# Five graph layers in one program: the next pass's weights and first rows prepared in the last groups of the pass ahead, and three steps of VectorE in another order

## The chip, the core and the metric

One Trainium2 chip, of which the program uses one core. Its engines are TensorE (PE), VectorE (DVE), ScalarE (ACT), GpSimd (POOL) and SyncE (SP); SP only issues DMA transfers here. The metric is the device time of one execution in microseconds (us), lower is better.

## What is computed

`x` has 128 graphs of 64 nodes with 384 features, fp32; `adj` is 128 x 64 x 64. Four layers follow one another, each `x = layernorm(x + layer(x, adj))`:

```python
# layer 0 and layer 3: attention with 12 heads, a bias from adj, an output projection
scores = einsum(q, k) * scale + bias            # bias = adj + adj in layer 0, adj in layer 3
p = softmax(where(any(scores != 0), scores, -inf)); out = einsum(p, v) @ Wo.T + bo
# layer 1: masked attention, with row biases for q, k, v, no output projection
scores = where(adj > 0, einsum(q, k) / sqrt(32) + beta * adj, -9e15)
out = einsum(softmax(scores), v)
# layer 2: twice (two sets of weights), then the residual and layernorm of the layer
attn = normalised(softmax(h @ h.T / sqrt(384)) * adj)
ctx = (attn * upper) @ (h @ Wl.T + bl) + diag(attn) * (h @ Ws.T + bs) + (attn * lower) @ (h @ Wr.T + br)
h = relu(layernorm(ctx) * g + b)
```

## The kernel before

The 8192 rows (128 graphs x 64 nodes) are 16 groups of 512 rows; a group is four units of 128 rows, two graphs each. The program runs five passes over all rows, each storing its result to HBM for the next: l0 (attention), l1 (masked attention), l20 and l21 (the two halves of layer 2, `digcn_pass`; only l21 has `ends`, the layer's residual and second norm), and l3 (attention). l0 and l3 are the same code with `wo`, the output projection; l1 has none.

Each fp32 operand of a large product is held in two parts, a rounded high part and the rest, and each product is three matmuls over these (`SPLIT`). For the rows: DVE transposes 128 x 512 tiles from `xa` to `xF` (L743 in the attention passes, L1363 in the digcn passes), ACT makes the high part (L591, L1239), POOL the low part (L379, L1099), three tiles a group. For the weights, nine tiles of 128 x 384 in each pass: DVE transposes them out of `raw` (L727, L1348; not in l1, whose weights come in the right form), ACT makes the high part (L583, L1231), DVE the low part (L733, L1352).

A pass is one block with a queue written by hand for each engine; `over_groups` calls `group` for the 16 groups, and writes the first two and the last two out. Order on an engine is that of the code; engines wait for one another by semaphores that count. At its start a pass of before fetches and splits the rows of groups 0 and 1 and its weights; it ends with a barrier of all engines (L883, L1529), behind which the next pass begins. The raw weights of the next pass are fetched by DMA in the pass ahead.

In an attention pass the projections of group i+1 stand on PE between the steps of group i (`BETWEEN`). One unit's chain is: PE scores (L478); DVE adds the bias (L770), takes the maximum (L777) and, with `wo`, the minimum (L779); POOL subtracts (L396); ACT takes the exponential (L663); DVE sums (L784); PE transposes (L491) and multiplies with v (L512 or L516). With `wo`, ACT and DVE split the outcome into oT (L817 is its low part), PE multiplies by Wo (L531), and DVE adds the residual (L828) with the statistics (L832, L835). Without `wo`, DVE scales (L813), POOL adds the residual (L373). `normed` on ACT, three instructions, makes the normalised row in all three passes.

In l1 DVE also makes the bias of the next group in unit 2 (`edges`: L757, L759), and POOL adds the bias of v (L354).

In a digcn pass PE multiplies the rows with themselves (L1152) for the attention of group i+1, and projects LEFT, RIGHT and SELF for each unit (L1179). DVE's `attention` has steps 0 to 4; step 3 is L1397 and L1403, whose outcome `wide` PE transposes (L1163); step 4 is L1408 and L1410. All of them are for the next group and stand in units 1 to 3. `context` on DVE is L1432 (in l21), L1437, L1440; `itself`, in l20 only, is L1417, which empties the SELF bank. POOL's L1106 adds the row biases of the LEFT and RIGHT projections. In l21 the bias of SELF is a row that ACT rounds (L1301, L1302), DVE splits (L1489) and PE adds (L1185).

## Time and profile before

| | |
|---|---|
| time before, median of 3 runs | 2734.35 us (2733.89 to 2734.68) |
| profiled execution, its own time | 2734.95 us |
| its span, mean granted clock | 2733.2 us, 0.964 |
| busy over the span: PE, DVE, ACT, POOL | 90%, 73%, 62%, 72% |

Time is in microseconds from the span's start. A clock of 1.00 is 2.4 GHz, one of 0.50 is 1.2 GHz. The engine's idle time in a row is that just before the instruction, and the releaser is what ended it; a row with "x3" stands for three instructions with nothing else between them on that engine. SPq rows are the issues of DMA transfers. The passes run, roughly, from 24 to 636 us (l0), 640 to 1175 (l1), 1180 to 1591 (l20), 1595 to 2100 (l21) and 2105 to the end (l3).

### The profile page before, as it was taken

The page shows a single profiled execution, that of the slowest core. Times are in us where ns is not written, and L with a number is a line of the kernel's source. Part 1 is how long each engine was busy: PE and PEld are TensorE (multiplying, and loading weights), DVE is VectorE, ACT ScalarE, POOL GpSimd, SP SyncE. Part 2 cuts the span into 40 slices and gives each one's busy share as a digit, 9 for nine tenths or more (in the row PEclk, how much of TensorE's full clock was granted, in tenths as well). Part 3 has the DMA queues.
Part 4 walks back from the last instruction along what each step waited for, and adds up shares of the span by engine and source line. Part 5 has one row for each costly group of instructions (what it writes and reads, how often), then busy time and mean ns, then how long its engine had stood idle before and what let it go on. Part 6 is the DMA issues. An engine that isn't in the chain of part 4 may idle for free. (4 is left out here: it accounts for less than half of the span.)

```text
span 2733.2 us, 65211 instructions
## 1 busy us (share of the span) xinstructions
PE 2471.4 (90%) x21554; PEld 2108.1 (77%) x21554; DVE 1992.3 (73%) x3475; ACT 1689.4 (62%) x3606; POOL 1969.1 (72%) x2189
## 2 busy tenths in 40 slices
PE   6999999985999999869999968888885999999997
PEld 4888888874877777758888857777774888888886
DVE  4777777773677667668888858888787577777776
ACT  4667666664777777745454445555654576666665
POOL 3888788873777777756666647777775588878786
PEclk9999999997999999979999989999997999999998
DMA  7222223115233332172333163333324222232211
GB/s 128 62 71 70 70 65 73 44 50 101 69 84 80 79 81 67 55 129 63 75 73 69 39 120 75 92 79 79 79 70 91 53 69 71 68 72 68 59 46 50
DMA packets 320602, 200.71 MB, mean 73 GB/s; under 512 B 243426, under 2 KB 320484, under 8 KB 320484
## 3 DMA queue, kind: packets, MB, share of 16 engines
q1 hardware_dynamic: 320484, 199.21, 31.6%
q8 instruction: 66, 1.08, 0.2%
q14 instruction: 52, 0.43, 0.1%
HBM read 136.22 MB, written 62.91 MB: 73 GB/s over the span
## 5 line engine op out<-in xcount | busy, mean ns | idle before, releaser
L1179 PE MATMUL l_ps_h<-l_w,l_hT 128*128 128x384 f32 x3456 | 672.0, 347 | 2.3 <-issue 2.3
L457 PE MATMUL l_ps_p<-l_xT,l_w 128*128 128x512 f32 x2304 | 598.3, 407 | 83.3 <-POOL l_xT L379 76.8
L1179 PEld LDWEIGHTS l_ps_h<-l_w,l_hT 128*128 128x128 f32 x3456 | 614.9, 193 | 63.3 <-issue 54.0
L457 PEld LDWEIGHTS l_ps_p<-l_xT,l_w 128*128 128x128 f32 x2304 | 426.3, 191 | 179.8 <-DVE l_w L733 51.7
L784 DVE TENSOR_REDUCE l_st<-l_pr 128x12 f32<-128x768 f32 x192 | 182.9, 953 | 348.7 <-ACT l_pr L663 348.7
L396 POOL TENSOR_TENSOR l_pr<-l_sc,l_st 128x768 f32<-128x768 f32 x192 | 285.1, 1485 | 172.2 <-DVE l_st L777 172.2
L1261 ACT ACTIVATE l_hlr<-l_ps_h 64x384 f32<-64x384 f32 x512 | 248.8, 486 | 196.8 <-PE l_ps_h L1179 190.0
L354 POOL TENSOR_TENSOR v<-v,l_bvs 128x768 f32<-128x768 f32 x192 | 356.2, 1855 | 0.0
L1106 POOL TENSOR_TENSOR l_hlr<-l_hlr,l_sides 128x768 f32<-128x768 f32 x128 | 246.7, 1928 | 125.6 <-ACT l_hlr L1261 125.4
L451 PE MATMUL l_ps_p<-l_w,l_xT 128*128 128x384 f32 x1584 | 312.6, 342 | 15.7 <-ACT v L622 14.8
L451 PEld LDWEIGHTS l_ps_p<-l_w,l_xT 128*128 128x128 f32 x1584 | 272.6, 188 | 25.3 <-ACT v L622 18.8
L531 PE MATMUL l_ps_y<-l_w,l_oT 128*128 128x384 f32 x1152 | 234.1, 348 | 43.7 <-DVE l_oT L817 39.9
L622 ACT ACTIVATE v<-l_ps_p 64x192 f32<-64x192 f32 x704 | 228.0, 324 | 55.0 <-PE l_ps_p L451 47.3
L531 PEld LDWEIGHTS l_ps_y<-l_w,l_oT 128*128 128x128 f32 x1152 | 205.7, 192 | 66.9 <-issue 63.4
L379 POOL TENSOR_TENSOR l_xT<-l_xF,l_xT 128x512 fp32r<-128x512 f32 x144 | 184.0, 1291 | 85.8 <-ACT l_xT L591 85.8
L405 POOL TENSOR_TENSOR l_pr<-l_pr,l_st 128x768 f32<-128x768 f32 x128 | 188.6, 1473 | 69.5 <-DVE l_st L795 69.5
L663 ACT ACTIVATE l_pr<-l_pr 128x768 f32<-128x768 f32 x192 | 162.2, 845 | 116.8 <-POOL l_pr L396 115.9
L770 DVE SCALAR_TENSOR_TENSOR l_sc<-l_ps_s,l_sbias 128x768 f32<-128x768 f32 x192 | 183.6, 956 | 34.0 <-PE l_ps_s L478 27.8
L777 DVE TENSOR_REDUCE l_st<-l_sc 128x12 f32<-128x768 f32 x192 | 183.0, 953 | 6.6
L658 ACT ACTIVATE l_pT<-l_ps_t 128x512 f32<-128x512 f32 (+1 forms) x384 | 167.4, 490 | 19.7 <-PE l_ps_t L491 13.7
L478 PE MATMUL l_ps_s<-l_k,l_qT 64*64 64x128 f32 x4608 | 172.7, 281 | 5.9 <-DVE l_sc L770 5.9
L478 PEld LDWEIGHTS l_ps_s<-l_k,l_qT 64*64 64x64 f32 x4608 | 125.7, 134 | 64.7 <-issue 58.0
(138 smaller groups left out, 4383.6 us busy)
## 6 DMA issues: line engine op xcount, KB each, us to landing
rows<-l_yo SPq DMA_DIRECT2D x256, 192.0 KB, 1.9
l_xa<-rows SPq DMA_DIRECT2D x256, 192.0 KB, 4.3
l_xr<-rows SPq DMA_DIRECT2D x192, 192.0 KB, 2.4
l_xa<-in_x SPq DMA_DIRECT2D x64, 192.0 KB, 4.3
l_xr<-in_x SPq DMA_DIRECT2D x64, 192.0 KB, 2.3
out<-l_yo SPq DMA_DIRECT2D x64, 192.0 KB, 1.9
l_edge<-in_adj SPq DMA_DIRECT2D x80, 128.0 KB, 2.4
raw<-in_L_gnn_Wq SPq DMA_DIRECT2D x12, 144.0 KB, 4.9
```

What stands on the lines that cost most here:

```text
L354: nc.gpsimd.tensor_tensor(got, got, bvs[:, :, :].unsqueeze(1).to_broadcast([P, GPU, PAIRS, 64]), ALU.add).then_inc(pool_v, 1)
L379: nc.gpsimd.tensor_tensor(xT[gpar][:, 1, t, :], xF[:, t, :], xT[gpar][:, 0, t, :].bitcast(F32), ALU.subtract).then_inc(low_x, 1)
L396: nc.gpsimd.tensor_tensor(pr[b][:, :, :], sc[b][:, :, :], st[b][:, 0, :].unsqueeze(2).to_broadcast([P, HEADS, NODES]), ALU.subtract).then_ ...
L405: nc.gpsimd.tensor_tensor(pr[b][:, :, :], pr[b][:, :, :], st[b][:, 5, :].unsqueeze(2).to_broadcast([P, HEADS, NODES]), ALU.mult).then_inc( ...
L451: last = nc.tensor.matmul(bank[:, :D], rows[:, l, t, o * P:(o + 1) * P], W[2][:, r, t, :], start=c + t == 0, stop=c == 2 and t == KT - 1)
L457: last = nc.tensor.matmul(bank[:, :], W[m][:, l, t, o * P:(o + 1) * P], rows[:, r, t, :], start=c + t == 0, stop=c == 2 and t == KT - 1)
L478: last = nc.tensor.matmul(logits[g * NODES:(g + 1) * NODES, h:h + 2, :NODES], qT[par][q, t, c:c + NODES], k2[par][q, t, :, c:c + NODES], s ...
L531: last = nc.tensor.matmul(ps_y[:, :D], oT[b][:, l, t, :], W[3][:, r, t, :], start=c + t == 0, stop=c == 2 and t == KT - 1)
L622: i = nc.scalar.activation(v2[gpar][64 * odd:64 * odd + 64, GPU * u + g2, :, 32 * odd:32 * odd + 32], got[:, :, odd, :], ACT.Copy)
L1106: nc.gpsimd.tensor_tensor(hlr[b][:, :, :], hlr[b][:, :, :], sides[:, :, :], ALU.add).then_inc(pool_h, 1)
L1179: last = nc.tensor.matmul(ps_h[m][:, :D], hT[gpar][:, l, t, s * P:(s + 1) * P], W[m][:, r, t, :], start=c + t == 0, stop=not (ends and m = ...
L1261: i = nc.scalar.activation(hlr[b][half * NODES:(half + 1) * NODES, g, :], ps_h[m][g * NODES:(g + 1) * NODES, :D], ACT.Copy)
```

## The change

What both kinds of pass share now lies in `Shared`: `W`, `xa`, `xF` (double-buffered in the attention passes too), `xT`, and the semaphores of this work, whose counts run on through all passes. A `Feed` describes what a pass is fed with: its rows, its weights, and the counts at its start.

- Rows. Groups 16 and 17 of a pass are groups 0 and 1 of the next. They are fetched, transposed and split in the usual places of groups 14 and 15. A pass from the second on no longer fetches or splits its first rows (of the six tiles all are done for l1 and l20; for l21 and l3 five are transposed and three split, the rest follow at the start).
- Weights. In the last group of an attention pass the nine tiles of the next pass are done three to a unit: DVE's transposes behind the softmax sum of units 0 to 2 (none for l1), ACT's high parts and DVE's low parts in units 1 to 3, with the banks of the projections. In a digcn pass each unit of groups 14 and 15 does one tile, the last unit two: DVE transposes at the unit's end, ACT follows, and DVE makes the low part at the head of the next unit. The two digcn passes have weight buffers of their own in turn. Wo stays where it was, at the start of l0 and l3.
- In l0 and l3 the minimum stands behind oT's low part in every unit.
- In l1 `normed` is one DVE instruction behind `low_part`, in place of three on ACT.
- In the digcn passes step 3 of `attention` stands ahead of `context` (l21) and of `itself` (l20). Step 4 stays.
- In l21 the rounding of the bias row is counted by its own semaphore.

```diff
+        self.W = [sb(f"w{m}", [P, 2, KT, D], F32R) for m in range(4)]
+        self.xa = [sb(f"xa{b}", [P, 4 * UNITS, D // 4]) for b in range(2)]
+        self.xF = [sb(f"xF{b}", [P, KT, ROWS]) for b in range(2)]
+        self.xT = [sb(f"xT{b}", [P, 2, KT, ROWS], F32R) for b in range(2)]
+        self.s_xa = [nc.alloc_semaphore(f"s_xa{b}") for b in range(2)]
+        self.dve_turn, self.act_x, self.low_x, self.dve_wt, self.act_w, self.dve_w = (
+            nc.alloc_semaphore(x) for x in ("dve_turn", "act_x", "low_x", "dve_wt", "act_w", "dve_w"))
...
+class Feed:
+
+
+    def __init__(self, k, src, mats, turned, W, turned_before, tiles_turned, tiles_split):
+        self.k, self.src_x, self.mats, self.turned, self.W = k, spread(src), mats, turned, W
+        self.rows_base, self.w_base, self.wt_base = KT * 16 * k, 3 * KT * k, 3 * KT * turned_before
+        self.tiles_turned, self.tiles_split = tiles_turned, tiles_split
...
+        def next_bank(step):
+            return (*ps_p, ps_y)[step % 3][:, :]
+
+        def has_rows(g):
+            return inside(g, groups + (2 if nxt else 0))
...
             def rows_in(g, gpar):
-                if not inside(g, groups):
-                    return
-                if counted(g - 1):
-                    sp.wait_ge(dve_turn, KT * (g - 1))
+                if not has_rows(g):
+                    return
+                if counted(rb + KT * (g - 1)):
+                    sp.wait_ge(dve_turn, rb + KT * (g - 1))
                 for j in range(4):
-                    sp.dma_start(xa[gpar][32 * j:32 * j + 32, :, :], src_x[g, j]).then_inc(s_xa[gpar], 16)
-
-            rows_in(0, 0)
-            rows_in(1, 1)
+                    part = nxt.src_x[g - groups, j] if isinstance(g, int) and g >= groups else me.src_x[g, j]
+                    sp.dma_start(xa[gpar][32 * j:32 * j + 32, :, :], part).then_inc(s_xa[gpar], 16)
+
+            if me.k == 0:
+                rows_in(0, 0)
...
-            shared.load(sp, next_mats, next_turned, lambda m: sp.wait_ge(dve_w, KT * min(m + 1, NM)))
+            if nxt:
+                shared.load(sp, nxt.mats, nxt.turned, lambda m: sp.wait_ge(dve_w, wb + KT * min(m + 1, 3)))
...
-            for step in range(KT):
-                weight_high(step)
+            if me.k == 0:
+                for step in range(KT):
+                    weight_high(me, step, w_bank(step))
             for t in range(KT):
                 rows_high(0, 0, t)
-            for step in range(KT, 3 * KT):
-                weight_high(step)
+            if me.k == 0:
+                for step in range(KT, steps):
+                    weight_high(me, step, w_bank(step))
             if row_bias_cols:
...
             def normed(n, count, b):
 
-                if not inside(n, units):
+                if not inside(n, units) or not wo:
...
+                    if nxt and s and isinstance(i, int) and i == groups - 1:
+                        act.wait_ge(pe_p, 10 * groups)
+                        for step in range(KT * (s - 1), KT * s):
+                            weight_high(nxt, step, next_bank(step))
...
+            def softmax_min(n, s):
+                b = s % 2
                 if wo:
                     nc.vector.tensor_reduce(st[b][:, 1, :], sc[b][:, :, :], AX.X, ALU.min).then_inc(dve_mn, 1)
...
+            def normed(n, count, b):
+                if not inside(n, units) or wo:
+                    return
+                dve.wait_ge(pool_rs, n + 1)
+                dve.wait_ge(dve_mv, n + 1)
+                if counted(16 * count):
+                    dve.wait_ge(s_out[b], 16 * count)
+                nc.vector.tensor_scalar(yo[b][:, :], res[b][:, :], ln[b][:, 6:7], ln[b][:, 9:10], ALU.subtract,
+                                        ALU.mult).then_inc(ready_y, 1)
...
+            if me.k == 0:
+                for t in range(KT):
+                    weight_turned(me, t, w_bank(t), 4)
+                for t in range(KT):
+                    weight_low(me, t, w_bank(t))
...
                     residual(n - 3, count, 1 - s % 2)
                     softmax_max(n, par, s)
                     low_part(n - 2, s % 2)
+                    softmax_min(n, s)
+                    normed(n - 3, count, 1 - s % 2)
                     if s == 2:
                         edges(i + 1, pair + (1 if par else 0), 1 - par)
                     softmax_sum(n, s)
                     for t in ((0, 1), (2,), (), ())[s]:
                         rows_turned(i + 2, par, t)
+                    if nxt and isinstance(i, int) and i == groups - 1:
+                        if s:
+                            for step in range(KT * (s - 1), KT * s):
+                                weight_low(nxt, step, next_bank(step))
+                        else:
+                            dve.wait_ge(act_v, units)
+                        if s < 3:
+                            for step in range(KT * s, KT * (s + 1)):
+                                weight_turned(nxt, step, next_bank(step), 3)
 
...
+        def next_step(i, s):
+
+            j = (i - groups + 2) * UNITS + s if isinstance(i, int) else -1
+            return () if j < 0 else (7, 8) if j == 7 else (j,)
...
                     left_right(n, b, RIGHT)
+                    for step in next_step(i, s):
+                        weight_high(step)
...
+            def weight_turned(step):
+                m, t = divmod(step, KT)
+                dve.wait_ge(s_raw[m], shared.loads[m])
+                if step >= 2:
+                    dve.wait_ge(dve_w, nxt.w_base + step - 1)
+                nc.vector.transpose(ps_w[step % 2][:, :D], blocks(raw[m])[:, :, 32 * t:32 * t + 32]).then_inc(dve_wt, 1)
+
+            def weight_low(step):
+                m, t = divmod(step, KT)
+                dve.wait_ge(act_w, nxt.w_base + step + 1)
+                nc.vector.tensor_tensor(nxt.W[m][:, 1, t, :], ps_w[step % 2][:, :D], nxt.W[m][:, 0, t, :].bitcast(F32),
+                                        ALU.subtract).then_inc(dve_w, 1)
...
-            weights(LEFT)
             dve.wait_ge(c_mask, masks)
-            for t in range(KT):
-                rows_turned(0, 0, t)
-            weights(RIGHT)
-            attention(0, 0, 0)
-            weights(SELF)
-            for step in range(1, 5):
+            for step in range(5):
                 attention(0, 0, step)
-            rows_turned(1, 1, 0)
-            rows_turned(1, 1, 1)
             dve.wait_ge(s_small, 16 * n_small)
             if ends:
-                dve.wait_ge(act_w, steps + 1)
+                dve.wait_ge(c_row, 2)
                 nc.vector.tensor_tensor(bias[32:33, :], brow[32:33, :], bround[32:33, :].bitcast(F32),
                                         ALU.subtract).then_inc(c_row, 1)
 
...
                     before = (i, par, s - 1) if s else (i - 1, 1 - par, UNITS - 1)
+                    for step in next_step(i, s - 1) if s else next_step(i - 1, UNITS - 1):
+                        weight_low(step)
+                    if s == 3:
+                        attention(i + 1, 1 - par, 3)
                     if ends:
                         context(n - 1, *before)
                     itself(n - 1, 1 - b)
                     if s == 3:
-                        attention(i + 1, 1 - par, 3)
                         attention(i + 1, 1 - par, 4)
                     if ends:
...
+                    for step in next_step(i, s):
+                        weight_turned(step)
...
+    feeds = [Feed(0, x, w0, True, shared.W, 0, 0, 0), Feed(1, kept[0], w1, False, shared.W, 1, 6, 6),
+             Feed(2, kept[1], w2[0], True, shared.W, 1, 6, 6), Feed(3, kept[2], w2[1], True, None, 2, 5, 3),
+             Feed(4, kept[3], w3, True, shared.W, 3, 5, 3)]
...
```

The new order of DVE is shown at three places. First, l0 in a steady unit: `l_sc` are the scores, `l_st` the statistics, `l_oT` the split output. Before:

```order
L770 SCALAR_TENSOR_TENSOR l_sc<-l_ps_s,l_sbias 128x768
L777 TENSOR_REDUCE l_st<-l_sc 128x12
L779 TENSOR_REDUCE l_st<-l_sc 128x12
L817 TENSOR_TENSOR l_oT<-l_ps_o,l_oT 128x384
L784 TENSOR_REDUCE l_st<-l_pr 128x12
L789 SCALAR_TENSOR_TENSOR l_st<-l_st 128x12
L792 RECIPROCAL l_st<-l_st 128x12
```

After, at the same place:

```order
L803 SCALAR_TENSOR_TENSOR l_sc<-l_ps_s,l_sbias 128x768
L810 TENSOR_REDUCE l_st<-l_sc 128x12
L853 TENSOR_TENSOR l_oT<-l_ps_o,l_oT 128x384
L815 TENSOR_REDUCE l_st<-l_sc 128x12
L820 TENSOR_REDUCE l_st<-l_pr 128x12
L825 SCALAR_TENSOR_TENSOR l_st<-l_st 128x12
L828 RECIPROCAL l_st<-l_st 128x12
```

The minimum (L779, now L815) has changed places with the low part (L817, now L853).

Second, l21 in the last unit of a group, DVE: `l_u` is the attention being made for the next group, `l_c` the context of the unit before. Before:

```order
L1389 SCALAR_TENSOR_TENSOR l_st<-l_st 128x4
L1392 RECIPROCAL l_st<-l_st 128x4
L1423 REGISTER_ALU
L1431 REGISTER_ALU
L1432 TENSOR_TENSOR l_c<-l_ps_c,l_hs 128x384
L1437 BN_STATS l_ln<-l_c 128x6
L1440 BN_AGGR l_ln<-l_ln 128x2
L1397 TENSOR_TENSOR l_attn<-l_u,l_st 128x256
L1403 TENSOR_TENSOR l_wide<-l_attn,l_halves 128x512
L1408 TENSOR_REDUCE l_st<-l_u 128x4
L1410 TENSOR_TENSOR l_diag<-l_st 128x4
```

After:

```order
L1451 SCALAR_TENSOR_TENSOR l_st<-l_st 128x4
L1454 RECIPROCAL l_st<-l_st 128x4
L1459 TENSOR_TENSOR l_attn<-l_u,l_st 128x256
L1465 TENSOR_TENSOR l_wide<-l_attn,l_halves 128x512
L1485 REGISTER_ALU
L1493 REGISTER_ALU
L1494 TENSOR_TENSOR l_c<-l_ps_c,l_hs 128x384
L1499 BN_STATS l_ln<-l_c 128x6
L1502 BN_AGGR l_ln<-l_ln 128x2
L1470 TENSOR_REDUCE l_st<-l_u 128x4
L1472 TENSOR_TENSOR l_diag<-l_st 128x4
```

The rows on `l_attn` and `l_wide` now stand ahead of the three of the context; the two that make `l_diag` stay behind them.

Third, the end of l1 on DVE. Before, the last units of l1 are followed by the head of l20 (`raw`, `l_w`: weights; `l_xa`, `l_hF`: rows):

```order
L813 TENSOR_TENSOR l_scaled<-l_ps_o,l_st 128x384
L832 BN_STATS l_ln<-l_res 128x6
L835 BN_AGGR l_ln<-l_ln 128x2
L832 BN_STATS l_ln<-l_res 128x6
L835 BN_AGGR l_ln<-l_ln 128x2
L184 UNCONDITIONAL_BRANCH
L1340 UNCONDITIONAL_BRANCH
L1348 STREAM_TRANSPOSE l_ps_w<-raw 128x384 x2
L1348 STREAM_TRANSPOSE l_ps_a<-raw 128x384
L1352 TENSOR_TENSOR l_w<-l_ps_w,l_w 128x384 x2
L1352 TENSOR_TENSOR l_w<-l_ps_a,l_w 128x384
L1363 STREAM_TRANSPOSE l_hF<-l_xa 128x512 x3
```

After, a unit of the last group of l1 holds such work, for `xF` and `w`, of which l20 reads:

```order
L810 TENSOR_REDUCE l_st<-l_sc 128x12
L849 TENSOR_TENSOR l_scaled<-l_ps_o,l_st 128x384
L880 TENSOR_SCALAR l_yo<-l_res,l_ln 128x384
L820 TENSOR_REDUCE l_st<-l_pr 128x12
L835 RECIPROCAL l_st<-l_st 128x2x3x2
L776 STREAM_TRANSPOSE xF<-xa 128x512
L761 TENSOR_TENSOR w<-l_ps_p,w 128x384 x2
L761 TENSOR_TENSOR w<-l_ps_y,w 128x384
L755 STREAM_TRANSPOSE l_ps_p<-raw 128x384 x2
L755 STREAM_TRANSPOSE l_ps_y<-raw 128x384
L868 BN_STATS l_ln<-l_res 128x6
L871 BN_AGGR l_ln<-l_ln 128x2
```

Behind the reciprocal of the softmax stand one row transpose, the low parts of three weights and the transposes of three more; `l_yo` is the normalised row, now made here.

## Rows read from the trace of the kernel before

**Rows 1.** Windows: start:end, length, busy us of each engine (instructions), PEclk, DMA share, GB/s.
```profile
85.00:600.00 515.00, 501.91 (x4832) 431.27 (x4832) 386.20 (x674) 350.88 (x785) 413.81 (x378) 1.00 0.25 63
...
700.00:1140.00 440.00, 417.80 (x4386) 345.63 (x4389) 306.81 (x468) 334.19 (x741) 336.14 (x325) 1.00 0.30 75
...
1199.00:1570.00 371.00, 371.00 (x2649) 322.19 (x2647) 305.80 (x553) 185.47 (x376) 242.10 (x256) 1.00 0.31 69
...
1615.00:2080.00 465.00, 415.82 (x2759) 357.32 (x2757) 366.86 (x671) 270.48 (x504) 359.49 (x616) 0.95 0.34 81
```

**Rows 2.** Waits of PE, 85 to 560 us: us in total, times, longest.
```profile
PE l_ps_y L531 <- DVE l_oT L817: 11.3, 13, 1.0
```

**Rows 3.** Timeline, seam l0 to l1: start, us, instruction [idle before, releaser].
```profile
640.38 5.28 SPq L287 DMA_DIRECT2D l_xa<-rows  x8
...
652.21 0.36 DVE L841 TENSOR_SCALAR l_kbm<-l_qkb,even_odd 128x3 f32<-128x3 f32 x2 [11.29 <-DMA l_betas<-in_L_gnn_beta]
...
659.51 5.81 PE L457 MATMUL l_ps_p<-l_xT,l_w 128*128 128x512 f32 x15 [25.65 <-POOL l_xT L379]
```

**Rows 4.** Timelines of the seams l1 to l20, l20 to l21, l21 to l3.
```profile
1179.81 4.77 SPq L988 DMA_DIRECT2D l_xa<-rows  x8
...
1188.12 2.83 PE L1152 MATMUL l_ps_u<-l_hF 128*64 128x64 f32 x48 [17.57 <-DVE l_hF L1363]
...
1610.64 0.53 ACT L1301 ACTIVATE l_bias<-l_brow 1x384 fp32r<-1x384 f32 x1 [1.45 <-DMA l_shift<-in_L_gnn_ln_b]
...
1614.64 0.45 PE L1185 MATMUL l_ps_h<-l_bias,pick 128*128 128x384 f32 x1 [2.72 <-DVE l_bias L1489]
...
2105.05 4.85 SPq L287 DMA_DIRECT2D l_xa<-rows  x8
...
2116.51 2.04 PE L457 MATMUL l_ps_p<-l_xT,l_w 128*128 128x512 f32 x4 [27.41 <-POOL l_xT L379]
```

**Rows 5.** Waits of PE, 1620 to 2060 us (l21).
```profile
PE l_ps_a L1163 <- DVE l_wide L1403: 41.5, 14, 4.0
```

**Rows 6.** Timeline of l21, the last unit of two groups in succession.
```profile
1907.96 1.81 POOL L1106 TENSOR_TENSOR l_hlr<-l_hlr,l_sides 128x768 f32<-128x768 f32 x1
...
1909.60 0.46 DVE L1397 TENSOR_TENSOR l_attn<-l_u,l_st 128x256 f32<-128x256 f32 x1
...
1911.74 3.39 PE L1179 MATMUL l_ps_h<-l_w,l_hT 128*128 128x384 f32 x18 [0.25 <-issue]
...
1939.19 0.56 DVE L1432 TENSOR_TENSOR l_c<-l_ps_c,l_hs 128x384 f32<-128x384 f32 x1
...
1940.55 0.42 DVE L1397 TENSOR_TENSOR l_attn<-l_u,l_st 128x256 f32<-128x256 f32 x1
...
1942.53 5.64 PE L1179 MATMUL l_ps_h<-l_w,l_hT 128*128 128x384 f32 x18
```

**Rows 7.** Groups of instructions, 85 to 560 us: busy, mean ns, idle before.
```profile
L379 POOL TENSOR_TENSOR l_xT<-l_xF,l_xT 128x512 fp32r<-128x512 f32 x39 | 49.8, 1290 | 0.0
...
L779 DVE TENSOR_REDUCE l_st<-l_sc 128x12 f32<-128x768 f32 x52 | 49.0, 943 | 0.0
```

**Rows 8.** Timeline of l20, last unit of a group, DVE and PE.
```profile
1412.28 0.69 DVE L1403 TENSOR_TENSOR l_wide<-l_attn,l_halves 128x512 f32<-128x512 f32 x1
...
1413.22 1.86 PE L1179 MATMUL l_ps_h<-l_w,l_hT 128*128 128x384 f32 x9
```

**Rows 9.** The page's costliest groups: busy, mean ns, idle before.
```profile
L784 DVE TENSOR_REDUCE l_st<-l_pr 128x12 f32<-128x768 f32 x192 | 182.9, 953 | 348.7 <-ACT l_pr L663 348.7
```

**Rows 10.** Timeline of l1, third unit of a group, DVE and POOL.
```profile
945.42 1.58 DVE L759 SCALAR_TENSOR_TENSOR l_sbias<-l_edge,l_betas,l_off 128x256 f32<-128x256 f32 x1
...
946.68 2.01 POOL L354 TENSOR_TENSOR v<-v,l_bvs 128x768 f32<-128x768 f32 x1
...
949.70 0.56 DVE L832 BATCH_NORM_STATS2 l_ln<-l_res 128x6 f32<-128x384 f32 x1 [0.86 <-POOL l_res L373]
```

**Rows 11.** Tile raw, 560 to 800 us: count, ns min/median/max, first and last.
```profile
L733 DVE TENSOR_TENSOR l_w<-raw,l_w x9: 542/551/1614, 652.5 to 661.1; 128x384 fp32r<-128x384 f32 x9
```

More of the change, by code:

```diff
@@ L185, in attention_pass @@
         a = Pass(nc, ctx, tag)
-        W = [a.sb(f"w{m}", [P, 2, KT, D], F32R) for m in range(NM)]
+        W = me.W
+        rb, wb = me.rows_base, me.w_base
         ident, raw, s_raw = shared.ident, shared.raw, shared.s_raw
@@ L647, in _ @@
                     rows_high(1, 1, pos - 2)
-            for step in range(3 * KT, steps):
-                weight_high(step)
+            if wo:
+                for t in range(KT):
+                    output_weight_high(t)
             def probs_T(n, b):
@@ L855, in _ @@
             edges(0, 0, 0)
-            for step in range(3 * KT, steps):
-                weight_low(step)
+            if wo:
+                for t in range(KT):
+                    output_weight_low(t)
             ni = [0]
@@ L903, in digcn_pass @@
         a = Pass(nc, ctx, tag)
-        W = [a.sb(f"w{m}", [P, 2, KT, D], F32R) for m in range(3)]
+        W = me.W
+        rb, wb = me.rows_base, me.w_base
         ident, ones, raw, s_raw = shared.ident, shared.ones, shared.raw, shared.s_raw
@@ L1229, in weight_high @@
                 m, t = divmod(step, KT)
[L1230 to L1231 removed]
+                act.wait_ge(dve_wt, nxt.wt_base + step + 1)
+                nc.scalar.activation(nxt.W[m][:, 0, t, :], ps_w[step % 2][:, :D], ACT.Copy).then_inc(act_w, 1)
             def rows_high(g, gpar, t):
[L1234 removed]
+                if not has_rows(g) or isinstance(g, int) and KT * g + t < me.tiles_split:
                     return
[L1236 removed]
+                act.wait_ge(dve_turn, rb + KT * g + t + 1)
                 if counted(g - 1):
@@ L1520, in _ @@
             over_groups(dve, groups, group)
+            for step in next_step(groups - 1, UNITS - 1):
+                weight_low(step)
             itself(units - 1, 1)
```

248 lines of the change are left out of this document (112 added, 136 removed).

## The prediction

> **What bounds the kernel now.** I read the windows of the trace first, because the mean over the page hides that the five passes have different limits [rows 1]. In l0 (and in l3, which is the same code) PE is busy 501.91 of 515 us, at granted clock 1.00, the higher of its two levels. In l20 it is busy 371.00 of 371. In both only work taken from PE, or a wait of PE, is worth anything. In l1 PE is busy 417.80 of 440 and in l21 415.82 of 465, where the clock is 0.95: there PE waits for others. Then I read the waits of PE in l0: 13 waits for DVE's low part of oT, 11.3 us together, none over 1.0 [rows 2]. The rest of PE's idle time stands at the four seams between passes, so the timeline of each seam comes next [rows 3, 4]: rows are fetched (8 DMA issues, about 5 us), transposed and split before the first matmul. In l21 the table of waits names one wait alone, for L1403, 41.5 us in 14 waits [rows 5]; its timeline [rows 6] shows how it comes about.
>
> The sum is made against the profiled execution: 2734.95 us, of which 2733.2 are span. That lies 0.6 us over the median of the runs, 2734.35. A change of about 0.2%, 5.5 us, is what a measurement of this kernel can tell from none.
>
> **Seams.** The first matmul of l1 comes at 659.51, after 25.65 us of waiting for the low part of the rows [rows 3]. Now weights and rows are there when the pass opens, at 640.38, where SP issues its first DMA. PE can start at about 640.6: 18.9 us sooner. What could be late next is kbm, the bias of k: DVE makes it at 652.21, having waited 11.29 us for the betas, which SP issues behind the 5.28 us of row DMAs. With those gone it comes at 652.21 - 5.28 = 646.9. ACT needs it only once it has emptied the three q tiles; those are 27 matmuls, and 15 of them took 5.81 us, so they keep PE until about 650. No new wait: -18.9.
>
> l1 to l20: products at 1188.12 move to just behind 1179.81, 8.2 to 8.5 us: -8.5 [rows 4]. l20 to l21: the end of the first SELF projection, L1185, waits for the bias row until 1614.64. ACT rounds that row at 1610.64, which waited for the small DMAs. These stand on SP behind eight row DMAs, which take 4.8 us to issue (4.77 in l20's row), and come that much sooner, so ACT's part moves to 1605.8. Behind it stand a second ACT row and DVE's low part, which no longer queue behind row transposes; about 1.5 us for both gives 1607.3: -7.3. l21 to l3: 2116.51 moves to 2105.2: -11.3. Seams together: -46.0. The bounds are 40 (a few us of start-up that I don't see, at each seam about 1.5) and 48 (l21 not held by its bias row).
>
> **l0 and l3, the min moved behind oT's low part.** Nothing is removed. L779 takes 0.94 us and stands ahead of L817 in DVE's order [rows 7]; PE waits for L817 0.87 us a group (11.3/13), at most 1.0 [rows 2]. With L779 behind it, L817 comes up to 0.94 sooner. PE has almost nothing else to wait for, so I take 0.7 a group over 30 groups: -21. Ends: -27 (all 0.87 and the peeled groups) and 0 (ACT's high part, which L817 needs, turns out as late as the min). A loss is excluded by order: if L817 must wait, the min starts no later than L817's end in the old order plus its own time, so L784 behind the two starts no later than before.
>
> **l21, attention rows ahead of the context step.** Before, L1397 and L1403 stand behind L1432, L1437 and L1440. In one kind of group (lower half of the group, [rows 6]) L1432 starts at 1939.19 and L1397 at 1940.55: 1.36 us that the move gives. PE waited there the 4.0 us that [rows 5] have as the longest, and its next 18 matmuls took 5.64 us instead of 3.39, at the lower clock level. With the wait down to 2.64, closer to the other kind's (41.5 - 7 x 4.0 over the other 7 is 1.9), the clock may stay up: 2.25 us more. That is 1.36 to 3.6 us, and up to 4.1 with the transposes in front, which I put at 0.5. In the other kind of group (upper half) L1397 starts at 1909.60, ahead of the end of POOL's L1106 (1907.96 + 1.81 = 1909.77). Moved forward it has two SBUF inputs under a POOL operation that began first, and I expect it to be held to the same moment: 0. Half of each is 0.7 to 2.05 us a group; I take 1.45 over 15 groups: -22. Ends: -41, if the other kind gains its 1.3 us too, and -5, if the context, which comes 1.2 us later, becomes what PE or the normalisation waits for.
>
> The Trainium skill, "SBUF — State Buffer", section "Who interferes with whom", says that a VectorE instruction with two SBUF inputs and a GpSimd instruction that reads SBUF exclude each other, and that whichever issues first has the port for its whole length. By that rule the kind in the upper half gains nothing; without it the term would be -31 rather than -22. The rows agree: L1397 takes 0.46 us and was seen to end only behind L1106.
>
> **l20, the same move ahead of L1417.** PE is never idle there [rows 1]. L1417 empties the bank for the SELF projection, which starts at 1413.22. DVE runs L1417, L1397 and L1403 back to back, and the last of them ends at 1412.28 + 0.69 = 1412.97; in the new order L1417 ends there instead, 0.25 us ahead of PE [rows 8]. Nothing gained, nothing lost: 0; if L1397 is held by L1106 the margin is gone, at up to 1 us a group: +15.
>
> **l1, the last normalisation on DVE instead of ACT.** One DVE instruction of about 0.55 us a unit more, three on ACT less. ACT is not what the loop waits for; DVE, POOL and PE take turns. In three units of four DVE has idle time where it goes: before L784 it waits for ACT's exponential, 348.7 us over 192 units, 1.8 us each [rows 9]. In unit 2 it stands ahead of L757 and L759; the latter now takes 1.58 us because POOL's L396 holds it [rows 10], and it would slip under the next POOL operation, L354, which runs from 946.68 for 2.01 us. The sum L784 behind it then comes about 1.4 us later, of which 0.86 is covered: L832 sits idle that long for POOL's L373. So about 0.5 us a group over 15: +7. Ends: -3 (PE's waits for ACT shorten and count) and +20 (1.4 us uncovered).
>
> **What the seams' work costs where it now stands.** It is not gone: 9 split weights a seam at 0.55 us on DVE (x9, up to 1.61 when held by POOL), in three seams 9 transposes too, and 6 row tiles with a POOL part of 1.29 us each [rows 7, 11]. It stands in the last one or two groups of each pass. In l0: 9 x 0.55 + 6 x 1.29 = 12.7 us on the two engines that carry the softmax loop; I take +12. In l1: 18 weight operations, 9.9 us, and POOL's 7.7, partly side by side: +12. In l20 DVE is busy 305.80 of 371, which leaves 4 us free in each group (371 us hold 15, of 24.7 each), so of 9.9 + 5 us in two groups most is hidden: +4. In l21 PE waits for DVE, but the weights are spread over eight units: +5. Sum +33; ends +12 (ACT and POOL parts beside PE's own waits) and +60 (every operation on the chain, some held).
>
> **Sum.** -46 - 21 - 22 + 0 + 7 + 33 = -49 us: 2734.95 - 49 = 2686.
>
> **Rivals.**
> 1. Full gain: clock stays up in all of l21 and the moved work is hidden: -46 - 27 - 35 + 3 + 17 = -88, 2647 us. For it: 41.5 us of waits in l21 stand on one DVE instruction. Against: the softmax loop of the last groups is what they are bound by, and the added work is on it.
> 2. Attention rows gain little, because they are held by L1106 in both kinds of groups, or since the context is late in their place: -46 - 21 - 4 + 10 + 33 = -28, 2707 us.
> 3. Seams paid twice: the work of preparation costs in the tails what it saved, every piece of it on the chain: -46 - 21 - 22 + 7 + 60 = -22, 2713 us.
> 4. Slower: DVE instructions with two inputs that were added or moved are held past the end of one POOL operation and through the next one too. In l1 the normalisation then ends behind L354 (2 us later) in each of 60 units, which pushes L832 by about 0.7 us in three of four and 1.7 in the fourth: +57; in l20 L1417 is late by 1 to 1.6 us a group: +20; in l21 the move gains nothing; the 63 weight operations take 1.6 us instead of 0.55: +66. These are 143 us; with half of them on the chain the sum is -46 - 21 + 33 + 72 = +38, 2773 us. It decides from 0.3 us on the chain for each of the some 170 instructions added or moved (49/170). Against it: L759 had to wait for the POOL operation ahead of L354, but ended at 945.42 + 1.58 = 947.00 with L354 begun at 946.68; it wasn't held through that one too [rows 10].
>    The Trainium skill's rule quoted above would have it that such a hold ends with the one instruction that began first, so it speaks against this rival.
> 5. The change does nothing at the seams: each pass still begins with the barrier and small DMAs, which could be what counts. Against: only the low part of the rows and, in l21, the bias row are named as what PE waits for.
>
> **How the numbers follow.** Forecast (2668 to 2702) 0.55; full gain 0.12; attention rows little 0.20; seams paid twice 0.07; slower 0.04; nothing at the seams 0.02 (-21 - 22 + 7 + 33 = -3, 2732 us, within 0.2%). Of seams paid twice I give 0.01 to an end within 0.2%. So faster 0.93, same 0.03, slower 0.04. The range takes in the forecast, the second and third rivals, and the nearer part of the first: 2655 to 2714.
>
> **What would show it.** Right: first matmul of l1 less than 2 us behind SP's first DMA; no wait over 0.3 us for oT's low part in l0; waits for the attention rows in l21 between 1 and 2.7 us, with 18 matmuls in 3.4 us in most groups; PE busy all of l20. Wrong: a new wait of PE for L1417's or L1432's successor; l1's groups longer by over 1 us; the last group of a pass longer by over 12 us; the clock in l21 still at its lower level in every second group.

## The result and the profile after

The changed kernel takes 2724.52 us (median of 6 runs, 2722.33 to 2726.38), the kernel before 2734.59 in the same comparison: a ratio of 0.9961, 95% interval 0.9948 to 0.9973. It is faster by 10 us, not by 49, and lies outside the range of 2655 to 2714. The profiled execution has a span of 2724.7 us (before 2733.2), granted clock 0.963. One of the six executions of e9 below was slow (3039.0 us at clock 0.744) and is left out of its median.

The windows of the changed kernel answer to [rows 1] (l0; l1; l20; l21), in stretches chosen from its own timeline:

```profile
85.00:555.00 470.00, 461.86 (x4451) 400.06 (x4450) 372.84 (x624) 324.62 (x729) 384.96 (x352) 1.00 0.29 69
...
668.90:1136.20 467.30, 439.80 (x4566) 361.79 (x4566) 405.33 (x547) 289.24 (x601) 360.27 (x337) 1.00 0.32 77
...
1192.00:1560.90 368.90, 366.06 (x2612) 317.78 (x2610) 305.16 (x546) 181.37 (x368) 235.61 (x248) 1.00 0.34 74
1719.00:2021.30 302.30, 271.04 (x1801) 231.63 (x1801) 260.59 (x452) 178.65 (x330) 236.15 (x410) 0.95 0.35 82
```

In l0 PE is now busy 98.3% (97.5% before). In l21 PE is still idle a tenth of the time and the clock still 0.95: the part on which 22 us of the forecast stood has hardly changed, and DVE is busy 86% there (79% before). The waits of PE over the whole program say where the idle time is now (total, times, longest):

```profile
PE l_ps_a L1229 <- DVE l_wide L1465: 32.3, 13, 2.9
PE l_ps_y L550 <- DVE l_oT L853: 31.1, 33, 3.8
...
PE l_ps_p L476 <- PEq L1590: 18.8, 1, 18.8
PE l_ps_t L510 <- POOL l_pr L425: 17.2, 18, 2.6
...
PE l_ps_h L1245 <- ACT l_hs L1385: 13.9, 6, 3.2
...
PE l_ps_u L1218 <- PEq L944: 9.9, 1, 9.9
PE l_ps_u L1218 <- PEq L1590: 9.4, 1, 9.4
...
PE l_ps_p L476 <- PEq L944: 6.7, 1, 6.7
```

The four rows with PEq are the seams (from the last matmul of a pass to the first of the next): the first matmul now waits for the barrier (L944, L1590) and for nothing else. The wait for L1385, the SELF copy of ACT in l21, is new. The starts themselves, from the timeline, answer to [rows 3, 4]:

```profile
646.24 7.19 PE L476 MATMUL l_ps_p<-xT,w 128*128 128x512 f32 x18 [6.75 <-PEq L944]
...
1183.70 2.83 PE L1218 MATMUL l_ps_u<-xF 128*64 128x64 f32 x48 [9.91 <-PEq L944]
...
1608.57 0.69 PE L1251 MATMUL l_ps_h<-l_bias,pick 128*128 128x384 f32 x1 [3.05 <-DVE l_bias L1543]
...
2114.14 6.18 PE L476 MATMUL l_ps_p<-xT,w 128*128 128x512 f32 x14 [18.84 <-PEq L1590]
```

From the timelines of both kernels I took the start of the first score addition of each group (attention passes) or of the transposes (digcn passes), and the first and last matmul of each pass. A tail is the stretch from such a start in the last group to the last matmul of the pass. The differences add up to the difference of the spans, -8.6 us:

| stretch | before | after | us |
|---|---|---|---|
| l0, program's start to the first scores of group 15 (period 36.62, now 36.19) | 593.6 | 586.7 | -6.9 |
| l0, tail | 40.3 | 52.8 | +12.5 |
| seam l0/l1 | 25.65 | 6.75 | -18.9 |
| l1, first matmul to first scores | 22.2 | 22.7 | +0.5 |
| l1, first scores to group 15 (period 31.12, now 31.46) | 460.3 | 467.3 | +7.0 |
| l1, tail | 28.6 | 37.6 | +9.0 |
| seam l1/l20 | 17.57 | 9.91 | -7.7 |
| l20, first matmul to the transposes for the last group (period 24.67 in both) | 374.8 | 377.2 | +2.4 |
| l20, tail | 24.7 | 27.0 | +2.2 |
| seam l20/l21 | 15.87 | 9.40 | -6.5 |
| l21, first matmul to first transposes | 11.4 | 11.8 | +0.4 |
| l21, first transposes to those of the last group but one (period 30.7, now 30.2) | 418.8 | 412.2 | -6.6 |
| l21, the last group and the tail | 55.4 | 74.0 | +18.7 |
| seam l21/l3 | 27.41 | 18.84 | -8.6 |
| l3, first matmul to first scores | 25.7 | 25.9 | +0.2 |
| l3, first scores to the end | 591.0 | 584.7 | -6.4 |

### The profile page after: what moved, and what is told of

Same layout as the page of the kernel before. It is cut to its first block and busy times, and to the rows that moved or that the text cites. A ratio compares the mean times of both kernels' runs of the same rounds, so it can differ in the third digit from the quotient of the medians.

```text
span 2724.7 us, 65081 instructions
## 1 busy us (share of the span) xinstructions
PE 2481.2 (91%) x21554; PEld 2121.9 (78%) x21554; DVE 2141.1 (79%) x3539; ACT 1614.8 (59%) x3414; POOL 1973.6 (72%) x2189
## 5 line engine op out<-in xcount | busy, mean ns | idle before, releaser
L476 PE MATMUL l_ps_p<-xT,w 128*128 128x512 f32 x2304 | 593.6, 404 | 71.8 <-POOL xT L399 23.8
L476 PEld LDWEIGHTS l_ps_p<-xT,w 128*128 128x128 f32 x2304 | 425.5, 191 | 167.6 <-issue 42.9
L1245 PE MATMUL l_ps_h<-second,xT 128*128 128x384 f32 x1728 | 352.4, 356 | 14.5 <-ACT l_hs L1385 13.9
L1245 PEld LDWEIGHTS l_ps_h<-second,xT 128*128 128x128 f32 x1728 | 319.8, 200 | 45.7 <-issue 25.8
L1245 PE MATMUL l_ps_h<-w,xT 128*128 128x384 f32 x1728 | 324.9, 342 | 2.4 <-DVE l_hs L1479 2.4
L1245 PEld LDWEIGHTS l_ps_h<-w,xT 128*128 128x128 f32 x1728 | 299.6, 189 | 32.6 <-DVE l_hs L1479 21.9
L470 PE MATMUL l_ps_p<-w,xT 128*128 128x384 f32 x1584 | 313.7, 342 | 3.6 <-ACT v L643 3.0
L470 PEld LDWEIGHTS l_ps_p<-w,xT 128*128 128x128 f32 x1584 | 273.6, 188 | 13.3 <-ACT v L643 7.0
L550 PE MATMUL l_ps_y<-w,l_oT 128*128 128x384 f32 x1152 | 236.4, 351 | 36.2 <-DVE l_oT L853 31.1
L550 PEld LDWEIGHTS l_ps_y<-w,l_oT 128*128 128x128 f32 x1152 | 210.1, 195 | 55.0 <-issue 50.5
```

What stands on the lines that cost most here:

```text
L470: last = nc.tensor.matmul(bank[:, :D], rows[:, l, t, o * P:(o + 1) * P], W[2][:, r, t, :], start=c + t == 0, stop=c == 2 and t == KT - 1)
L476: last = nc.tensor.matmul(bank[:, :], W[m][:, l, t, o * P:(o + 1) * P], rows[:, r, t, :], start=c + t == 0, stop=c == 2 and t == KT - 1)
L550: last = nc.tensor.matmul(ps_y[:, :D], oT[b][:, l, t, :], W[3][:, r, t, :], start=c + t == 0, stop=c == 2 and t == KT - 1)
L1245: last = nc.tensor.matmul(ps_h[m][:, :D], hT[gpar][:, l, t, s * P:(s + 1) * P], W[m][:, r, t, :], start=c + t == 0, stop=not (ends and m = ...
```

## The experiments

Times are medians; the kernel before, run beside each, was between 2733.75 and 2735.69 us. Ratios are to it. Spans and stretches are those of each kernel's profiled execution.

**e1: attention rows back behind the context.**

```diff
-                    if s == 3:
-                        attention(i + 1, 1 - par, 3)
                     if ends:
                         context(n - 1, *before)
                     itself(n - 1, 1 - b)
                     if s == 3:
+                        attention(i + 1, 1 - par, 3)
                         attention(i + 1, 1 - par, 4)
```

> The changed kernel with step 3 of DVE's attention back behind the context step (l21) and behind itself (l20). My theory: moved forward, the attention multiplication is held by POOL's addition of the row biases in every group, so the move is worth little. Then the period of l21 goes from 30.2 back to 30.7 us a group, some 6 to 7 us in all, l20's first group gives 2 us back, and the kernel takes about 2729 us. Rival, the step of the prediction: the move gives 22 us and something else took 16 of them, then 2746 us.

Measured 2716.95 us, ratio 0.9940 (0.9926 to 0.9954): undoing the move makes the changed kernel 7.6 us faster. Both expectations had the wrong sign. The hold itself is there. These are rows of the table of instructions over ten groups of l21, first of the changed kernel (busy us, mean ns of one, idle us before):

```profile
L1459 DVE TENSOR_TENSOR l_attn<-l_u,l_st 128x256 f32<-128x256 f32 x10 | 14.0, 1396 | 0.3
L1465 DVE TENSOR_TENSOR l_wide<-l_attn,l_halves 128x512 f32<-128x512 f32 x11 | 12.5, 1136 | 0.4
```

and of e1:

```profile
L1465 DVE TENSOR_TENSOR l_wide<-l_attn,l_halves 128x512 f32<-128x512 f32 x10 | 7.0, 696 | 0.3
L1459 DVE TENSOR_TENSOR l_attn<-l_u,l_st 128x256 f32<-128x256 f32 x10 | 4.4, 442 | 0.0
```

Moved forward, the two take 2.5 us instead of 1.1. The timeline of one group of the changed kernel shows why:

```profile
1867.69 1.81 POOL L1172 TENSOR_TENSOR l_hlr<-l_hlr,l_sides 128x768 f32<-128x768 f32 x1
1868.01 1.78 DVE L1459 TENSOR_TENSOR l_attn<-l_u,l_st 128x256 f32<-128x256 f32 x1
1869.82 0.69 DVE L1465 TENSOR_TENSOR l_wide<-l_attn,l_halves 128x512 f32<-128x512 f32 x1
...
1870.57 0.88 PE L1229 MATMUL l_ps_a<-ident,l_wide 128*128 128x128 f32 x4 [2.29 <-DVE l_wide L1465]
...
1871.10 4.84 PE L1245 MATMUL l_ps_h<-second,xT 128*128 128x384 f32 x18
```

L1459 begins 0.3 us behind POOL's addition and ends 0.3 us behind its end, so PE waits 2.3 us, and the context begins 2.4 us behind the start of L1459 instead of ahead of it. In nine of the twelve steady groups (the fourth to the fifteenth of a pass's sixteen transposes) L1459 is held like this (1.8 to 1.9 us); in the other three POOL's addition begins just ahead of L1465, and that one takes 2.32 us. That is what the Trainium skill, "SBUF — State Buffer", section "Who interferes with whom", says of a VectorE instruction with two SBUF inputs beside a GpSimd one that reads SBUF. This leaves a question: with the old order e1 runs 29.7 us a group in l21, and the kernel before, in the same order, 30.7; e10 below answers that.

**e5: the whole attention chain earlier.**

```diff
+                    if s == 2:
+                        attention(i + 1, 1 - par, 1)
+                        attention(i + 1, 1 - par, 2)
+                        attention(i + 1, 1 - par, 3)
                     if s >= 2:
                         shift_by[0] = 2
                         rows_turned(i + 2, par, s - 2)
```

(and step 3 no longer in unit 3.)

> The changed kernel with steps 1 to 3 of DVE's attention in unit 2 ahead of the row transpose, in both digcn passes. Theory (hold): the attention multiplication now starts about 0.7 us earlier, ahead of POOL's addition of the row biases, and takes 0.45 us instead of 1.4; PE's wait for it falls from 2.4 us a group to under 1, l21's period from 30.2 to 28.5 or less, and the kernel from 2724.5 to about 2700 us. Rival (late by itself): the wait comes from where the chain of the softmax stands, not from the hold; then step 1 or 2 waits for ACT or POOL, DVE blocks, and the period stays within 0.3 us of 30.2.

Measured 2703.45 us, ratio 0.9882 (0.9867 to 0.9897): 21 us under the changed kernel. The period of l21 is 28.5 us, the clock of the stretch 0.99. The waits of PE between 1640 and 2000 us:

```profile
PE l_ps_u L1218 <- DVE xF L1425: 21.3, 13, 1.9
PE l_ps_a L1229 <- DVE l_wide L1465: 7.9, 13, 1.2
```

and the multiplication now lies ahead of POOL's addition:

```profile
L1459 DVE TENSOR_TENSOR l_attn<-l_u,l_st 128x256 f32<-128x256 f32 x10 | 4.2, 424 | 0.3
```

Standing ahead of one row transpose of 0.71 us was enough to take it from 1396 to 424 ns: in most groups POOL's addition now begins 1.16 us behind its start, not 0.3 us ahead. (In one steady group of twelve L1465 is still held, 2.35 us.) The 18 matmuls behind the transposes take 3.4 us in all twelve. The hold alone doesn't make all of the gain: e1 has neither multiplication held in its steady groups, and runs 29.7 us a group with waits of 2.3 to 2.4 us. The other 1.2 us come with the place ahead of the context, where PE's wait is 0.6 us and the granted clock 0.99 (e1: 0.96); how much is wait and how much clock was not separated. What is late next is the row transpose for the products, 1.6 us a group; and the last group is longer, 38.2 us.

**e6: PE's transposes in the next unit.**

```diff
                     project(n, i, par, s, RIGHT)
+                    if s == 0 and not (isinstance(n, int) and n == 0):
+                        attention_T(i)
                     context(n - 1, ppar, ps)
...
-                    if s == 3:
-                        attention_T(i + 1)
```

> The changed kernel with PE's transposes of the attention (and ACT's copy of them) one unit later: in unit 0 of the next group, behind the RIGHT projection, where the attention rows are long there. Theory: PE's wait of 2.4 us a group and the lower clock behind it are gone; DVE, busy 26 of 30.2 us with its holds, is next: period of l21 about 28 us, kernel 2724.5 - 2.2 x 14 = 2694 us. Rival (DVE or POOL is the bound already): the wait only moves, to PE's wait for the row biases or for the SELF copy, and the period stays above 29.7: 2718 us or more.

Measured 2723.39 us, ratio 0.9959 (0.9946 to 0.9973), period 30.3 us. My theory fell here: PE's wait for `wide` is gone and others stand in its place.

```profile
PE l_ps_u L1218 <- DVE xF L1425: 18.7, 11, 2.1
PE l_ps_h L1245 <- ACT l_hlr L1327: 15.3, 12, 2.0
```

A hold is still in every steady group: L1451, a tiny instruction ahead of L1459 (L1389 in the kernel before), takes 1.6 to 1.7 us in eight of twelve, L1465 2.2 to 2.4 in the other four. So taking away this one wait of PE brought nothing; e5, which takes the hold out of all but one of them, helped. That DVE's own loop sets the pace in e6 is the likely reason and was not tested by itself.

**e4: ACT makes a weight's high part one unit later** (and DVE its low part at the end of that unit).

```diff
-                    for step in next_step(i, s):
+                    for step in next_step(i, s - 1) if s else next_step(i - 1, UNITS - 1):
                         weight_high(step)
```

> The changed kernel, where in groups 14 and 15 of l20 and l21 ACT makes the high part of a weight one unit later than DVE transposed it, and DVE the low part at the end of that unit. Theory: in the changed kernel ACT stands in front of the weight that DVE transposes only at the end of the same unit, so the SELF copy behind it is late and PE waits up to 3.2 us a unit, 18 us in all in l21's tail. Without that wait the tail of l21 gets 10 to 15 us shorter: 2710 to 2715 us, and PE's waits for the copy (13.9 us) are gone. Rival: the tail is long because DVE has 18 more instructions there, wherever they stand: then at most 3 us.

Measured 2707.35 us, ratio 0.9909 (0.9896 to 0.9923): 17 us under the changed kernel. In the changed kernel, timeline of the last groups of l21:

```profile
2051.60 0.55 DVE L1409 STREAM_TRANSPOSE l_ps_w<-raw 128x384 f32<-128x384 f32 x1
2052.18 0.49 ACT L1297 ACTIVATE w<-l_ps_w 128x384 fp32r<-128x384 f32 x1 [5.40 <-DVE l_ps_w L1409]
...
2053.76 0.57 ACT L1385 ACTIVATE l_hs<-l_ps_h,l_diag 128x384 f32<-128x384 f32 x1
...
2054.38 1.96 PE L1245 MATMUL l_ps_h<-second,xT 128*128 128x384 f32 x7 [2.36 <-ACT l_hs L1385]
```

ACT stands 5.40 us in front of a weight that DVE transposes at the unit's end; the SELF copy is queued behind, and PE waits for the copy. With the edit no such wait is left: the step from the transposes of group 14 to those of 15 falls from 35.8 to 30.3 us, and from there to l3's first matmul from 57.0 to 47.3, less than the 54.3 of before. Against before, l21's last group and tail are then 3.4 us longer, not 18.7: ACT's place in the queue cost 15 us, DVE's 18 instructions with the rest 3.4.

**e2 and e3: the other two reorderings undone one by one.** e2 puts `softmax_min` ahead of `low_part` again; e3 lets ACT's `normed` run in l1 too and DVE's return at once.

> The changed kernel with the minimum back ahead of oT's low part in l0 and l3. Theory: the move gives 0.4 to 0.55 us a group, since ACT's high part is itself late for the other half; so l0's period goes from 36.1 to 36.65 us and the kernel to about 2738 us. Rival, the prediction's term: 21 us, 2745 us.

Measured 2734.36 us, ratio 1.0004 (0.9995 to 1.0013): the move of the minimum is worth 9.8 us in the changed kernel; the period of l0 goes back to 36.55. In the changed kernel PE still waits 7.1 us in 12 waits for the low part between 80 and 555 us, 0.6 each against 0.87 [rows 2].

> The changed kernel with l1's last normalisation back on ACT, three instructions. Theory: DVE's extra instruction costs 0.35 us a group in the loop and more in the last group, where DVE also does the weights; then l1's period goes from 31.45 to 31.1 us and the kernel to 2714 to 2719 us. Rival: the l1 loop is slower because of the double-buffered transpose or something else in the pass, and DVE's instruction costs nothing: within 2 us of 2724.5.

Measured 2718.13 us, ratio 0.9944 (0.9931 to 0.9958): 6.4 us faster, the period of l1 31.1 us. DVE's single instruction costs what was expected.

**e7 and e8: the seams alone, and the reorderings alone.** e7 is the changed kernel with all three reorderings undone; e8 is the kernel before with the three.

> Only the preparation of weights and rows in the pass ahead: the changed kernel with all three reorderings undone. From the runs so far (attention back -7.5, normalisation back on ACT -6.4, minimum back +9.8, against 2724.5) the sum is 2720.4 us. Rival (they interact, since l21's period depends on when the pass starts): more than 5 us away from that.

Measured 2726.85 us, ratio 0.9966 (0.9954 to 0.9979), 6.4 us over the sum: the parts interact.

> Only the three reorderings, on the kernel before. By the differences of the other runs: attention +7.5, normalisation +6 (less the 2 us of the last group, which has no weight work here), minimum -9.8: 2734.3 + 2 = 2736 us. If l21's period falls to 30.2 by the move of the attention rows alone, as the profiles of the kernel before and the changed one seem to say, it is 2734.3 - 7 + 4 - 10 = 2721 us.

Measured 2717.39 us, ratio 0.9932 (0.9919 to 0.9946). Alone, the seams give 8.8 us and the reorderings 18.3; together they give 10. The l21 period was 30.7 us in the kernel before, 29.9 in e7, 30.2 in e8. By the stretches of the table above, e7 saves 42.2 us of idle time at the four seams and pays 41.4 for it in the four tails (with l21's last group); its l21, from the first transposes to those of the last group but one, is 9.7 us shorter, although e7 doesn't change the steady code there. So what the seams gain, the tails take back, and e7's gain stands in l21's period.

**e10 and e12: a delay at the start of l21.** Nothing is added but eight small memsets, in e10 on the kernel before, in e12 on e7:

```diff
+                for j in range(8):
+                    nc.vector.memset(idle[:, :], 0.0).then_inc(c_idle, 1)
+                    dve.wait_ge(c_idle, j + 1)
                 nc.vector.tensor_tensor(bias[32:33, :], brow[32:33, :], bround[32:33, :].bitcast(F32),
```

> The kernel before, with eight small memsets of DVE ahead of the bias row at the start of l21, some 1.5 to 2 us, and nothing else. Theory (phase): l21's steady period depends on where the pass begins against the clock's changes and POOL's instructions, since the seams-only kernel, whose steady code is the same, ran 29.9 us a group where the kernel before ran 30.7. Then the delay changes the period by over 0.3 us in one way or the other and the alternation of 4.0 and 2.33 us of waiting goes. Rival (the seams' code changed the loop, by other buffers and semaphores): the period stays 30.7 and the kernel gets 1.5 to 2 us slower.

The memsets take 1.45 us, and the kernel takes 2725.5 us, ratio 0.9971 (0.9959 to 0.9983): 8 us faster than without them. The transposes of l21 in the kernel before, in successive groups:

```profile
1787.95 0.66 PE L1163 MATMUL l_ps_a<-ident,l_wide 128*128 128x128 f32 x4 [2.33 <-DVE l_wide L1403]
...
1818.87 1.11 PE L1163 MATMUL l_ps_a<-ident,l_wide 128*128 128x128 f32 x4 [4.03 <-DVE l_wide L1403]
...
1849.41 0.66 PE L1163 MATMUL l_ps_a<-ident,l_wide 128*128 128x128 f32 x4 [2.35 <-DVE l_wide L1403]
...
1880.34 1.11 PE L1163 MATMUL l_ps_a<-ident,l_wide 128*128 128x128 f32 x4 [4.03 <-DVE l_wide L1403]
```

and with the delay:

```profile
1786.02 0.66 PE L1165 MATMUL l_ps_a<-ident,l_wide 128*128 128x128 f32 x4 [2.38 <-DVE l_wide L1405]
...
1816.17 0.66 PE L1165 MATMUL l_ps_a<-ident,l_wide 128*128 128x128 f32 x4 [2.34 <-DVE l_wide L1405]
...
1844.87 0.66 PE L1165 MATMUL l_ps_a<-ident,l_wide 128*128 128x128 f32 x4 [2.35 <-DVE l_wide L1405]
...
1875.44 0.66 PE L1165 MATMUL l_ps_a<-ident,l_wide 128*128 128x128 f32 x4 [2.33 <-DVE l_wide L1405]
```

The alternation of the waits is gone; the period falls from 30.7 to 29.6 us. In the kernel before a tiny DVE instruction, L1389 on 128 x 4 elements, falls under POOL's addition in every second group. This is the kind of group with the long wait, in the lower half of [rows 6]:

```profile
1937.06 1.81 POOL L1106 TENSOR_TENSOR l_hlr<-l_hlr,l_sides 128x768 f32<-128x768 f32 x1
...
1937.32 1.58 DVE L1389 SCALAR_TENSOR_TENSOR l_st<-l_st 128x4 f32<-128x4 f32 x1
```

In the other kind L1389 is over before the addition begins and takes 0.16 us; the mean is 870 ns. The 18 matmuls behind the transposes take 5.65 us behind the wait of 4 us and 3.39 behind that of 2.33 (granted clock 0.91 and 0.98 in the group that follows). How one group sets up the next was not followed further. With the delay the same instruction takes 163 ns:

```profile
L1391 DVE SCALAR_TENSOR_TENSOR l_st<-l_st 128x4 f32<-128x4 f32 x10 | 1.6, 163 | 0.3
```

> The seams-only kernel with the same eight memsets at the same place. Phase: the period of l21 moves away from 29.9, possibly to 30.7 (then 2726.9 + 2 + 11 = 2740 us). Rival: it stays at 29.9 and the kernel gets 2 us slower, 2729 us.

Measured 2728.28 us, ratio 0.9978 (0.9970 to 0.9987), 1.4 us slower than e7, which is the length of the delay, but within the scatter of both. Its waits were 4.17 us once and 2.3 to 2.5 from then on, its period 30.1. So the same code can fall into the slow cadence or not, by where the pass starts; e7 is out of it with and without this one delay. Other delays were not tried.

**e9: e5, e4 and e3 together.**

> The changed kernel with three edits that helped singly: steps 1 to 3 of the attention ahead of the row transpose (measured -21 us), ACT's weight work a unit later (-17), l1's normalisation on ACT (-6). If each is a wait of its own they add: 2724.5 - 44 = 2680 us. If the first and the second share the tail of l21, where the first alone made the last group longer (38.2 us, not 35.8), it could be more than 44; if they meet the same bound there, less: 2690 us.

Measured 2681.34 us (five runs, 2674.59 to 2683.78), ratio 0.9811 (0.9798 to 0.9824). They add (2680 was the sum); the last group of l21 is back at 28.2 us.

**e11: e9, with the weights of l1 and l20 split at the start of these passes.** The rows of both still come from the pass ahead.

```diff
-                    if nxt and isinstance(i, int) and i == groups - 1:
+                    if nxt and nxt.k > 2 and isinstance(i, int) and i == groups - 1:
...
+            if me.k == 1:
+                for step in range(steps):
+                    weight_low(me, step, w_bank(step))
...
+            if me.k == 2:
+                own_weights(LEFT)
+                own_weights(RIGHT)
             dve.wait_ge(c_mask, masks)
             attention(0, 0, 0)
+            if me.k == 2:
+                own_weights(SELF)
```

> The combination (first kernel of this call) with the weights of l1 and l20 split at these passes' own start, while their rows still come from the pass ahead. Theory: in the last group of an attention pass each DVE operation is on the softmax chain, while at the start three weights delay PE by 2 to 3 us only, and the rest is hidden behind the first projections. Then l0's tail gets 5 us and l1's tail 8 us shorter, the starts 2.5 and 2 us longer: 8 us below the combination. Rival: the tails are long by the row tiles, and weights fit into their gaps: then it is 3 to 5 us above it.

Measured 2666.16 us, ratio 0.9748 (0.9735 to 0.9761), 15 us under e9 and 58 under the changed kernel: the fastest that I ran. From the start of l0's last group to l1's first matmul it is 50.9 us instead of 58.2; at the seam behind l1 40.1 instead of 47.8, and the start of l20 is only 0.6 us longer. (The two profiled spans differ by 6.7 us alone, since e9's is that of its fastest run: its l0 up to the last group, its steady l21 and its l3, which the edit doesn't touch, are 2.6, 3.1 and 2.1 us shorter than e11's.) The timeline of l1's start:

```profile
636.64 3.83 ACT L600 ACTIVATE w<-raw 128x384 fp32r<-128x384 f32 x9 [3.17 <-PEq L946]
637.20 4.31 DVE L761 TENSOR_TENSOR w<-raw,w 128x384 fp32r<-128x384 f32 x9
...
638.74 6.35 PE L476 MATMUL l_ps_p<-xT,w 128*128 128x512 f32 x18 [8.72 <-DVE w L761]
```

At the start, with DVE and ACT free, all nine weights take under 5 us and hold PE up for 2 (the barrier was passed at 636.6). In the last group of l0 they cost these 2 us and 7 more.

## Why the prediction was wrong

Two terms failed: l21's tail and l21's step. Two smaller ones, the minimum and the seams, were too large.

At the **seams** the mechanism was right, and the size nearly: -41.6 us of idle time at the four against -46. The bias row of l21 was ready for PE at 1608.57, where 1607.3 was forecast; that the two are so close is partly luck, since the forecast did not move the pass itself. Counted from the last matmul of l20 the row comes 6.3 us sooner, not 7.3. At l21/l3 the barrier itself is later behind the last matmul, 18.84 us, which I had put at the 16 of before.

The **tails** of the attention passes came as forecast: l0 +12.5 (+12), l1 +9.0 for its tail and 2.3 more in the group before it (+12). The tail of l20 was +2.2 (+4). The term that failed is l21's: +18.7 instead of +5. The sentence "the weights are spread over eight units" counted DVE's instructions and never asked in front of what ACT stands while it waits for them. e4 shows that wait and takes 17 us back, 15 of them here.

The **l21 step** is the second failure: -6.6 instead of -22. The term had two parts, a shorter wait and a clock that "may stay up". The wait did get shorter, by what the low end said: over the twelve steady groups PE's mean wait fell from 3.17 to 2.46 us, 0.7 a group (in e10, without the move, it is 2.35). The clock gave nothing back: the 18 matmuls behind the transposes took 4.52 us on average before (5.65 and 3.39 in turn) and 4.54 in the changed kernel, where the 2.25 us stood on 3.39 in every group.

The reading of the rows had missed what made the long wait, the hold of L1389 for 1.58 us. In such a group L1397, moved forward, is not held: e8 shows three of them, each with the tiny instruction at 1.67 us and PE's wait at 2.3 to 2.4. But in the steady groups of the changed kernel the tiny instruction starts ahead of POOL's addition and takes 0.16 us, and L1459 or L1465 is held instead. And the base against which I counted was a cadence of this one start: 1.1 of its 30.7 us goes away with a delay of 1.45 us (e10). Against the kernels without that cadence (29.7 in e1, 29.9 in e7, 29.6 in e10) the move costs 0.3 to 0.6 us a group. So the second rival was the true one for the move, and its reason (held in both kinds) too; the total was still off because of the tail.

The **minimum** was right in kind and too large: 9.8 us by e2 (13.3 by the segments of l0 and l3, with the program's start) instead of 21. The 0.87 us of waiting fell only to 0.6. The stated lower end, that ACT's high part is as late, would explain it; no run separates it. The **normalisation** in l1 was right: +7 forecast, 6.4 by e3. **l20** costs 2.4 us in its first groups, where I had 0; its steady loop is unchanged at 24.67, as the margin of 0.25 us said.

By the segments the sum was wrong by 40 us (-8.6 instead of -49): l21's step 15.4, l21's tail 13.7, the minimum 7.7 and the seams 4.4 make 41, and the small terms cancel.

## What to carry to other kernels

Work moved into another pass's last groups is priced on each engine by what is queued behind the instruction that waits, not by the busy time that it adds: put the consumer a unit behind its producer. Here the engines were free behind the barrier, and 2 us in the open cost less than the same work on the softmax chain (e11); without this the 42 us saved at the seams were paid back almost whole in the tails (e7). And before a reordering is credited with a change of a loop's period, run the old order from another start: 1.45 us of delay made this kernel 8 us faster.

## What I had not expected of the hardware

- The loop of l21 over four engines locks into a slow cadence that holds for the whole pass: waits of 4.03 and 2.33 us in turn, granted clock 0.94 over 307 us, against 2.3 to 2.4 each time and 0.96 with a delay of 1.45 us at the start. Which of hold and clock drives the lock was not separated.
- A DVE instruction on 128 x 4 elements took 1.58 us under a POOL addition and 0.16 us outside it: 870 ns on average in that cadence and 163 without it.
- Moving a two-input DVE instruction ahead of one transpose of 0.71 us took 0.97 us off its own mean duration (1396 to 424 ns). Each group got 1.7 us shorter with it, at a clock of 0.99 instead of 0.95.
